# Fused causal attention with routing: tiles that run on over batches, projections in six chunks, heads' loads in pieces

## The reference, cut to what matters

```python
for i, scale in enumerate((1, 2, 4)):            # second step: three scales, 8 heads
    xs = _avg_pool(x, scale) if scale > 1 else x
    q, k, v = jnp.split(_pwconv(_dwconv3x3(xs, dw_w[i], dw_b[i]), ...), 3, axis=1)
    out = softmax(einsum('bhdn,bhdm->bhnm', q + pos, k + pos) / 4) applied to v
# third step, on tokens t [4, 1024, 128], E = _ln_t(t)
W = einsum('bqd,bkd->bqk', E @ WQ.T, E @ WK.T) / sqrt(D)
M = where(W == 0, 0, tril)
x_exp = exp(W - max(W)) * M
t = t + (x_exp / (sum(x_exp) + EPS)) @ (E @ WV.T)
# fourth step, on x = _ln_t(t): the two best of 16 experts for each token
probs = softmax(x @ gate_w + gate_b); top_probs, top_idx = top_k(probs, 2)
t = t + sum over the two of weight * ((silu(x @ w1[e]) * (x @ w2[e])) @ w3[e])
# fifth step: attention with 8 heads on t as [2, 2048, 128], with a bias for each key column
```

## Time and profile before

| | before |
|---|---|
| median of 3 runs | 2147.29 us (2143.82 to 2149.95) |
| profiled execution, its own time | 2145.99 us |
| its span in the trace | 2144.1 us |
| PE busy | 1690.9 us (79% of the span) |
| DVE busy | 1399.3 us (65%) |
| ACT busy | 988.8 us (46%) |
| POOL busy | 257.6 us (12%) |
| DMA | 120.85 MB, mean 56 GB/s |
| mean granted clock of PE | 0.877 of full speed |

### The profile page before, as it was taken

One profiled execution on the slowest core, in us unless ns is written; L12 is line 12 of the kernel. 1 busy time (PEld: TensorE's weight loads), 2 busy tenths in 40 slices (PEclk: granted clock), 3 DMA queues, 4 the chain that ended last, 5 costly groups with the idle time before them and its releaser, 6 DMA issues. The chain is left out here.

```text
span 2144.1 us, 29779 instructions
## 1 busy us (share of the span) xinstructions
PE 1690.9 (79%) x9116; PEld 861.6 (40%) x9116; DVE 1399.3 (65%) x2755; ACT 988.8 (46%) x1816; POOL 257.6 (12%) x272
## 2 busy tenths in 40 slices
PE   4998697997999965758776199633799999975798
PEld 3776342222232222335555088512122232225476
DVE  4752698886888857356665134365788888845566
ACT  2554232565677742014533066423167776762243
POOL 1010201000000000000221545410001100100000
PEclk9999897898999977779987599857599999996799
DMA  2270174084234100103000131219123222200000
GB/s 81 103 121 1 36 149 167 1 122 78 51 62 65 25 11 1 29 27 98 17 16 13 43 109 56 66 49 217 59 31 65 58 50 51 50 14 1 20 0 39
DMA packets 114817, 120.85 MB, mean 56 GB/s; under 512 B 22980, under 2 KB 88972, under 8 KB 113692
## 3 DMA queue, kind: packets, MB, share of 16 engines
q1 hardware_dynamic: 101118, 102.07, 21.4%
q0 software_dynamic: 13600, 17.58, 2.8%
HBM read 77.38 MB, written 41.75 MB: 56 GB/s over the span
## 5 line engine op out<-in xcount | busy, mean ns | idle before, releaser
L953 DVE TENSOR_REDUCE heads_mx<-heads_n_bank 128x1 f32<-128x1024 f32 (+2 forms) x536 | 625.3, 1206 | 148.1 <-PE heads_n_bank L836 144.5
L934 ACT ACTIVATE heads_prob<-heads_t_bank 128x512 f32<-128x512 f32 (+1 forms) x1064 | 549.6, 601 | 365.1 <-PE heads_t_bank L855 364.8
L836 PE MATMUL heads_n_bank<-scale_ks,scale_qs 96*128 96x512 bf16 (+2 forms) x608 | 182.4, 395 | 41.1 <-PEq L43 24.7
L836 PE MATMUL heads_n_bank<-edge_ks,edge_qs 99*128 99x512 bf16 x512 | 164.2, 405 | 52.3 <-PEq L43 41.0
L855 PE MATMUL heads_t_bank<-scale_qs,scale_ks 99*128 99x512 bf16 (+2 forms) x608 | 173.1, 373 | 18.4 <-DMA scale_qs<-heads_mrows 14.9
L869 PE MATMUL heads_o_bank<-heads_prob,scale_vs 128*32 128x512 f32 (+2 forms) x1216 | 152.5, 576 | 13.0 <-DVE scale_out L971 11.7
L855 PE MATMUL heads_t_bank<-edge_qs,edge_ks 102*128 102x512 bf16 x512 | 155.3, 382 | 3.8 <-ACT heads_prob L934 3.8
L869 PE MATMUL heads_o_bank<-heads_prob,edge_vs 128*32 128x512 f32 x1024 | 136.4, 605 | 0.1
L836 PEld LDWEIGHTS heads_n_bank<-scale_ks,scale_qs 96*128 96x128 bf16 (+1 forms) x608 | 49.0, 105 | 185.8 <-issue 102.7
L836 PEld LDWEIGHTS heads_n_bank<-edge_ks,edge_qs 99*128 99x128 bf16 x512 | 39.5, 99 | 187.5 <-issue 117.1
L855 PEld LDWEIGHTS heads_t_bank<-scale_qs,scale_ks 99*128 99x128 bf16 (+1 forms) x608 | 58.5, 103 | 121.4 <-ACT heads_prob L934 55.9
(11 more groups left out here) (331 smaller groups left out, 2555.8 us busy)
## 6 DMA issues: line engine op xcount, KB each, us to landing
edges_text<-edges_targets SPq DMA_DIRECT2D x16, 512.0 KB, 3.7
scale_qs<-scale_q_parts SPq DMA_DIRECT2D x60, 128.0 KB, 5.1
scale_ks<-scale_k_parts SPq DMA_DIRECT2D x60, 128.0 KB, 7.2
heads_wide<-heads_inverse_d POOLq DMA_DIRECT2D x14, 512.0 KB, 8.5
edge_qs<-edge_q_parts SPq DMA_DIRECT2D x48, 128.0 KB, 4.3
edge_ks<-edge_k_parts SPq DMA_DIRECT2D x48, 128.0 KB, 6.4
routed_x<-attn_zeros SPq DMA_DIRECT2D x2, 2600.0 KB
experts_xs<-routed_x SPq DMA_DIRECT2D x16, 325.0 KB
```

The lines of the kernel that those rows point to most:

```text
L836: last = pe.matmul(ps[0:TN, at_:at_ + CH], query(b, slice(0, KB), s, h, j, t * TN, TN), key(b, slice(0, KB), s, j, i * CH, CH), start=True ...
L934: act.activation(to[:], t_ps[score_bank(of, place, g)[0]][0:TN, 0:HP * CH], ACT.Exp, scale=scale).then_inc(exped, 1)
L953: dve.tensor_reduce(mx[:, u % UC:u % UC + G], scores, AX.X, ALU.max, negate=True).then_inc(first_used, 1)
```

## The change

It has three places.

- **Scale 1's heads.** `HeadsEarly.load` now takes a part i and a half j: six q loads and v (j = 0), or six k loads (j = 1). `many_heads_attention` issues one such piece in each of g = 1 to 6 (the first four for the second scale, in two parts of two halves; then the third scale's).
- **Fifth step's heads.** `HeadsFirst.load` takes the half s. `head_inputs` loads half 0 alone; half 1 is loaded at the start of SP's queue in the attention stage.
- **attend_and_route.** Tiles are numbered g = 0 to 31 through all batches, and scores run two tiles ahead over a batch's end. q, k and v have two buffers each. The projections of the next batch are six chunks of 512 columns (q, q, k, k, v, v), made in the transposes' upper half while tiles 0 to 3 use only the lower, and copied out one by one (`keep_chunk`). PE's routing steps stand between a tile's scores and its value product, `turn_rows(., 0)` at the end of tile 1, and three of them a tile later than before. ACT's `normalise` is split over tiles 0, 1 and 2, and its other steps come a tile later too. DVE's `note_pages` runs at tile 1 of the batch after. The first projections wait for the three weight loads alone.

The diff, cut; of the two `load` functions and `attend_and_route` the removed lines, which stand in the listing above, are left out:

```diff
+    def load(self, sp, s):
+
+        self.load_qk(sp, 0, s, self.qk_loaded[s])
+        if s == 0 and self.bias_parts is not None:
+            sp.wait_ge(self.cleared, 2)
+            sp.dma_start(self.ks[STACK:STACK + 3, :], self.bias_parts.rearrange("l h n -> l (h n)")).then_inc(self.biased, 16)
+        self.load_v(sp, 0, s)
 
 
 class HeadsEarly:
@@ -635,14 +634,15 @@
         self.qk_loaded = [m.nc.alloc_semaphore(f"{name}_qk_loaded{i}") for i in range(B // self.LB)]
         self.v_loaded = [m.nc.alloc_semaphore(f"{name}_v_loaded{i}") for i in range(B // self.LB)]
 
+    def load(self, sp, i, j):
+
         n, LB = self.n, self.LB
+        part = slice(i * LB * n, (i + 1) * LB * n)
+        parts, dram, slots = ((self.qs, self.scratch.q, Q_PART), (self.ks, self.scratch.k, K_PART))[j]
+        for slot, level in enumerate(slots):
+            to = parts[slot * HD:(slot + 1) * HD, :].rearrange("r (g n) -> r g n", g=8)[:, :, part]
+            sp.dma_start(to, dram[level].rearrange("(g r) b n -> r g (b n)", r=HD)[:, :, part]).then_inc(self.qk_loaded[i], 16)
+        if j == 0:
             sp.dma_start(self.vs[:, i * LB:(i + 1) * LB], self.scratch.v[i * LB:(i + 1) * LB].rearrange("b p t c -> p b t c")).then_inc(self.v_loaded[i], 16)
...
             else:
+                if first.bias_parts is not None:
+                    first.load(sp, 1)
+                sp.wait_ge(cleared, 2)
+                pieces = [(one, i, j) for one in later for i in range(B // one.LB) for j in range(2)]
                 for g in range(2 * B):
                     b, s = g // 2, g % 2
                     rows(b, s * NH)
@@ -792,8 +796,9 @@
                     if 1 <= g < 2 * B - 1:
                         sp.wait_ge(kept, g * NH)
                         first.load_v(sp, (g + 1) // 2, (g + 1) % 2)
-                    if 1 <= g <= len(later):
-                        later[g - 1].load(sp)
+                    if 1 <= g <= len(pieces):
+                        one, i, j = pieces[g - 1]
+                        one.load(sp, i, j)
...
             for b in range(B):
                 sp.wait_ge(stored, b * 48 + 96)
                 if b == 2:
-                    first.load(sp)
+                    first.load(sp, 0)
...
-        q, k, v = sb("q", [P, N]), sb("k", [P, N]), sb("v", [P, T, C])
+        q, k, v = ([sb(f"{x}{i}", [P, N]) for i in range(2)] for x in "qkv")
-        LOADS = 7 * 16
+        LOADS = 4 * 16
+        WEIGHTS = 3 * 16
+        chunk_bank = lambda b, c: t_ps[:, 4:8, :] if b > 0 or c % 2 else t_ps[:, 0:4, :]
...
+            def project(b, c):
 
                 if b > 0:
+                    pe.wait_ge(turn_kept, (b - 1) * T)
+                    pe.wait_ge(proj_kept, 6 * b + c)
+                elif c >= 2:
+                    pe.wait_ge(proj_kept, c - 1)
+                to, part = chunk_bank(b, c), slice(c % 2 * 512, c % 2 * 512 + 512)
+                if c < 4:
+                    last = pe.matmul(to.rearrange("p t c -> p (t c)"), w[:, c // 2, :], m.xnT[:, b, part], start=True, stop=True)
+                else:
+                    for t in range(4):
+                        last = pe.matmul(to[:, t, :], m.xnT[:, b, part][:, t * P:(t + 1) * P], w[:, 2, :], start=True, stop=True)
+                last.then_inc(projected, 1)
+
+            def scores(g):
+                b, t = divmod(g, T)
+                if t == 0:
+                    pe.wait_ge(proj_kept, 6 * b + 4)
+                if g >= 2:
+                    pe.wait_ge(exped, g - 1)
+                    pe.wait_ge(masked, g - 1)
                 for h in range(2):
+                    last = pe.matmul(s_ps[g % 2][:, h * 512:(h + 1) * 512], q[b % 2][:, t * P:(t + 1) * P], k[b % 2][:, h * 512:(h + 1) * 512], start=True, stop=True)
                 last.then_inc(scored, 1)
 
+            def turn(g):
+                b, t = divmod(g, T)
+                pe.wait_ge(masked, g + 1)
+                if g >= 1:
+                    pe.wait_ge(turn_kept, g)
+                if t == 4 or g == 0:
+                    pe.wait_ge(proj_kept, 6 * min(b + 2, B) if g else 6)
                 for j in range(t + 1):
+                    last = pe.transpose(t_ps[:, j, :], prob[g % 2][:, j * P:(j + 1) * P], m.ident[:])
+                last.then_inc(turned, 1)
+
+            def mix(g):
+                b, t = divmod(g, T)
+                pe.wait_ge(turn_kept, g + 1)
+                if t == 0:
+                    pe.wait_ge(proj_kept, 6 * b + 6)
+                if g >= 1:
+                    pe.wait_ge(added, g)
+                for j in range(t + 1):
+                    last = pe.matmul(mix_ps[:], probT[g % 2][:, j, :], v[b % 2][:, j * P:(j + 1) * P], start=(j == 0), stop=(j == t))
                 last.then_inc(mixed, 1)
 
...
+            early, late = {0: 0, 1: 1, 2: 2, 3: 4}, {2: 3, 3: 5}
+            inside = {3: lambda f: turn_rows(f, 1), 4: gate_logits, 6: count_picks}
+
+            pe.wait_ge(w_loaded, WEIGHTS)
+            for c in range(6):
+                project(0, c)
             pe.wait_ge(loaded, LOADS)
             pe.wait_ge(prepared, 11)
+            scores(0)
+            scores(1)
+            for g in range(B * T):
+                b, t = divmod(g, T)
+                turn(g)
+                if g + 2 < B * T:
+                    scores(g + 2)
+                if b + 1 < B and t in early:
+                    project(b + 1, early[t])
+                if b >= 1 and t in inside:
+                    inside[t](b - 1)
+                mix(g)
+                if b + 1 < B and t in late:
+                    project(b + 1, late[t])
+                if b >= 1 and t == 1:
+                    turn_rows(b - 1, 0)
+            turn_rows(B - 1, 0)
+            for part in inside.values():
+                part(B - 1)
...
+            def keep_chunk(b, c):
+                act.wait_ge(projected, 6 * b + c + 1)
+                if b >= 2:
+                    act.wait_ge(scored, (b - 1) * T)
+                    act.wait_ge(mixed, (b - 1) * T)
+                to, part = (q, k, v)[c // 2][b % 2], slice(c % 2 * 512, c % 2 * 512 + 512)
+                act.activation(to[:, part], chunk_bank(b, c).rearrange("p t c -> p (t c)"), ACT.Copy, scale=scale if c < 2 else 1.0).then_inc(proj_kept, 1)
...
+            early, late = {0: 0, 1: 1, 2: 2, 3: 4}, {2: 3, 3: 5}
+            act.wait_ge(w_loaded, WEIGHTS)
+            for c in range(6):
+                keep_chunk(0, c)
+            exponentials(0)
+            exponentials(1)
+            for g in range(B * T):
+                b, t = divmod(g, T)
+                f = b - 1
+                if b >= 1 and t == 2:
+                    take_rows(f, 0)
+                keep_turned(g)
+                if b + 1 < B and t in early:
+                    keep_chunk(b + 1, early[t])
+                if g + 2 < B * T:
+                    exponentials(g + 2)
+                if b >= 1 and t == 3:
+                    take_rows(f, 1)
+                if b + 1 < B and t in late:
+                    keep_chunk(b + 1, late[t])
+                if b >= 1 and t == 0:
                     take_root(f)
+                    normalise(f, 0, 2)
+                elif b >= 1 and t == 1:
+                    normalise(f, 2, 4)
+                elif b >= 1 and t == 2:
+                    normalise(f, 4, 8)
+                elif b >= 1 and t == 4:
                     double(f)
+                elif b >= 1 and t == 5:
                     take_odds(f)
+                elif b >= 1 and t == 6:
                     arm(f)
+            take_root(B - 1)
+            normalise(B - 1, 0, 4)
+            take_rows(B - 1, 0)
+            normalise(B - 1, 4, 8)
+            take_rows(B - 1, 1)
+            double(B - 1)
+            take_odds(B - 1)
+            arm(B - 1)
...
+            beside = {0: (find_shift,), 4: (choose,), 5: (pick,), 6: (hand_out,), 7: (place_rows,)}
 
             step(dve.memset(epsb[:], 1e-5))
             dve.wait_ge(loaded, LOADS)
             dve.wait_ge(prepared, 11)
+            maximum(0)
+            maximum(1)
+            mask(0)
+            for g in range(B * T):
+                b, t = divmod(g, T)
+                if g + 1 < B * T:
+                    mask(g + 1)
+                if g + 2 < B * T:
+                    maximum(g + 2)
+                invert(g)
+                add_output(g)
+                if g >= 1:
+                    measure(g - 1)
                 if b >= 1:
+                    for part in beside.get(t, ()):
+                        part(b - 1)
+                if b >= 2 and t == 1:
+                    note_pages(b - 2)
             measure(B * T - 1)
+            note_pages(B - 2)
             for parts in beside.values():
                 for part in parts:
                     part(B - 1)
+            note_pages(B - 1)
```

More of the change, by code:

```diff
@@ L1118, in _ @@
                     sp.wait_ge(stored[0], 48)
-                    first.load(sp)
+                    for s in range(2):
```

(32 more changed lines are left out.)

155 lines of the change are left out of this document (33 added, 122 removed).

## The result

| | before | changed |
|---|---|---|
| median of 4 runs | 2145.64 us (2143.82 to 2149.95) | 2124.38 us (2123.56 to 2125.25) |
| ratio | | 0.9879, 95% interval 0.9859 to 0.9900 |
| span of the profiled execution | 2144.1 us | 2122.9 us |

What follows compares the result with a forecast made beforehand. It took load bursts and queued transfers to bound two places, and PE, then waits between engines, `attend_and_route`. Gains of 16.2, 13.5 and 17 us, less 1, took 2145.99 us to 2100.3, forecast 2100, range 2083 to 2119 (8 in 10).

Steps and rivals of the forecast that it cites:

- The sum: Whole kernel: gains of 16.2, 13.5 and 17 us, less 1 for costs to neighbours, 45.7 us in all.
- The fifth step's heads: Attention stage after the fifth step's inputs: half 1's loads are covered there and cost nothing; without cover, 13.7 us.
- Of the stall of 6.71 I take half.: `attend_and_route`, batches 2 and 3: half of DVE's 6.71 us stall stays, giving 50.85 us for each batch.
- the stall goes too: Rival, chance 0.10: the new order of `attend_and_route` removes the whole stall; gain 30 us, time 2087.
- Batches walked: `attend_and_route`, batches 1 to 3: tiles walked through the new orders, 46.8 us for batch 1, 50.85 each for 2 and 3.
- Batch 0 and the start: `attend_and_route`: the start gains 1.9 us; batch 0, now making batch 1's chunks, gives 3.4 us away.
- Tail: End of `attend_and_route`, 56.9 us from last slots to last scatter: kept, with ACT's copies costing 1 us.
- The stage as a whole: `attend_and_route`: gain of 17 us, bounds 4 and 33.
- the rival at 5: Rival, chance 0.13: the routing stage gains little, 5 us in place of 17, time 2112.
- ACT's table switches: Rival, chance 0.06: six switches in `attend_and_route` come onto the path at 1.28 us each, 7.7 us, time 2108.
- Scale 1's heads: Splitting the load burst removes PE's 14.86 us wait and gives clock back; gain 16.2 us, bounds 15 and 17.5.
- Fifth step's inputs: Loading half 0 alone ends the loads earlier, so the stage ends at 1498; gain 13.5 us, bounds 11 and 16.

Runs made afterwards that it cites:

- e2: Kernel before with only half 1's loads of the fifth step's heads moved behind that stage's begin; ratio 0.9931.
- e3: Kernel before with only the new `attend_and_route`; ratio 0.9991, fifth step's heads 420.1 us.
- e17: Kernel before with 46 idle waits on ACT's queue at the end of its part of `attend_and_route`; fifth step's heads 420.8 us.
- e5: Changed kernel with POOL's scatters of batches 0 and 1 put behind those of 2 and 3; batch 2 took 47.7 us, batch 3 41.6.
- e9: Kernel before with POOL's indirect DMAs of batches 0 and 1 paced two for each tile; 2121.88 us in one execution.
- e1: Kernel before with only the second and third scales' loads split into six pieces; ratio 0.9926.
- e15: Changed kernel with two indirect DMAs a tile and 1024 idle waits on ACT's queue; fifth step's heads 408.7 to 409.1 us (range shared with two other runs).
- e7: Changed kernel with POOL's indirect DMAs of batches 0 and 1 paced two for each tile; ratio 0.9804.
- e8: Changed kernel with two indirect DMAs for each tile and 96 idle waits on ACT's queue; median 2091.2 us, ratio 0.9737.

## Why the prediction was wrong

- **The sum left out a stage.** "The fifth step's heads" had a price only for half 1's loads (none, and none was seen: e2). The 7.8 us of ACT's two jumps back, which came with 24 more instructions in `attend_and_route` (e3, e17), stood in no term and no rival. This alone is a third of the miss. The trace of before shows no such wait, so it could not have been read there.
- **"Of the stall of 6.71 I take half."** It stayed whole: the burst costs 8.7 and 9.9 us in the changed kernel (e5), 10.3 and 11.3 in the old (e9). I reasoned that PE and ACT would work on meanwhile, but ACT is held by it too ([8.03] above), and PE behind it. The rival "the stall goes too" fell as well.
- **Batches walked.** Batch 1 was forecast 1.7 us shorter and is 1.6 shorter, but not all by the way I gave: DVE's waits for scores stayed at 8.0 us, the one at tile 2 being 4.1 where I had walked 2.4, and only those for value products fell. That the sum came out is in part luck. Batch 2 without the burst is 47.7 against 47.5 walked. Batch 3 without it is 41.6, since it makes no chunks for a next batch; I gave it the 47.5 of batch 2. That error of 5.9 hid nearly all of the stall's error there, 51.5 against 50.85, which is luck too.
- **Batch 0 and the start**: 1.8 us given away together against 3.4. **Tail**: 2.2 longer against 1. The stage as a whole gives 9.1 instead of 17, between the forecast and the rival at 5, though not for that rival's reasons; ACT's table switches are not seen as a cost either. The scatter of batch 2 began 11.4 us nearer to the norm's first product, not 18.
- **Scale 1's heads**: the mechanism was right, the size 12.6 for 16.2 in this trace, under the bound of 15. The two stretches from rows to rows with the wait and the half clock took 63.4 us (449.45 to 512.87 in the old timeline) and take 48.1 now (451.09 to 499.18), 15.3 less. But the next six took 144.4 and take 146.4, 2.0 more: single ones are up to 25.4 us long, where an undisturbed one takes 23.4, and three of the six carry a piece. I had taken off 1 us for all such. I had also read a half batch as 24 us; that is one stretch from rows to rows, and a half batch has two, some 47 us, so the pieces had more time than I gave them.
- **Fifth step's inputs**: 12.0 for 13.5; the three transfers took 0.5, 0.5 and 0.4 us longer than their rows said.
- The routed experts' 4.0 us stood in no term; e1 and e2 show nearly as much without the change (139.4 and 138.7), so this is at least mostly variation of that stage.

## What to carry to other kernels

When a kernel has loops in its instruction streams, a change that adds instructions ahead of one can cost or save time in it; compare a stage that the change doesn't touch first, look for waits named "issue" at equal distances, and try a few idle instructions before judging the change. Few, for they cost time of their own: with e15's 1024 waits the routed experts' first scatter came 39.3 us after the last one of the tail, and 18.4 with 512. A long burst of GpSimd's indirect DMAs was not free for the other engines here; where the data are not needed at once, try two for each tile. Give the last round of a pipelined loop its own price, for it carries no work for the next.

## What the runs showed of the hardware

- A jump back in ACT's stream, in a loop of 260 instructions, cost 4.3 to 4.9 us when the loop lay at one place or 128 instructions further, and nothing seen at moves of -24, 1, 2, 5, 25, 49, 129, 257 and 513 from it. Both jumps back of the loop over three batches waited, and 8 to 10 packets more of 8 KB were fetched in the stage.
- 16 indirect DMAs in a row, 1.26 us apart, came with a wait of DVE of 5.8 to 7.8 us that began 14 to 17 us after the first, in all 16 such bursts beside tiles, mostly on an instruction whose operands were ready. In the new order of tiles ACT stood still as well, for 6.2 to 8.1 us. Paced, two for each tile, they stopped neither (e7, e8, e9). What is held during it stays open: I did not measure it apart from this kernel.
